# Closes of quads put off to the end of the ranges, and two PSUM banks for the last sums

## The reference

```python
x = x + _L0_gnn_ref(_layernorm(x, axis=-1), src, dst, eps, W1, b1, W2, b2, gamma, beta)
x = x + _L0_ffn_ref(_layernorm(x, axis=-1)[None], gate_w, gate_b, w1, b1, w2, b2)[0]
# gnn: N=12500 nodes, E=200000 edges sorted by dst, D=256
neigh = jax.ops.segment_sum(node_feats[src], dst, num_segments=n)
h = (1.0 + eps) * node_feats + neigh
h = jax.nn.relu(h @ W1 + b1) @ W2 + b2          # 256 -> 512 -> 256
h = (h - mean) * rsqrt(var + BN_EPS) * gamma + beta   # over all nodes
# ffn: 8 experts, top-1 routing with a capacity, 256 -> 1024 -> 256
```

## Time and profile before

| | us |
|---|---|
| three executions | 2734.87, 2713.54, 2704.42 |
| median | 2713.54 |
| the profiled execution | 2722.03, its span 2720.3 |
| mean granted clock of TensorE | 0.858 |
| busy share | TensorE 68%, VectorE 51%, ScalarE 34%, GpSimd 57% |

### The profile page before, as it was taken

How to read it: one execution, slowest core, us unless ns; L and a number is a source line. 1 busy time by engine, 2 the same in 40 slices (tenths; PEclk the granted TensorE clock), 3 DMA queues, 4 the chain that set the end, 5 groups by cost and what they waited for, 6 DMA issues and landing times. The chain is left out here.

```text
span 2720.3 us, 35963 instructions
## 1 busy us (share of the span) xinstructions
PE 1843.1 (68%) x9315; PEld 1055.5 (39%) x9316; DVE 1386.2 (51%) x4375; ACT 911.7 (34%) x1518; POOL 1553.5 (57%) x1530
## 2 busy tenths in 40 slices
PE   0035456767858878676787765557764888979996
PEld 0012223333424444333343433334332555646664
DVE  8834544545544443334342322223664676858886
ACT  6811012323323333223221110102553555545553
POOL 1266665665565666556565654650445566847775
PEclk9966678888779889889898877788887999989998
DMA  7653335656658766575677422421662322140220
GB/s 228 226 186 106 108 86 178 206 187 193 222 181 264 241 201 203 189 232 192 211 250 252 137 79 69 128 82 58 212 196 87 101 81 79 34 144 22 92 89 21
DMA packets 228639, 411.91 MB, mean 151 GB/s; under 512 B 46469, under 2 KB 110299, under 8 KB 228406
## 3 DMA queue, kind: packets, MB, share of 16 engines
q1 hardware_dynamic: 164742, 243.58, 27.4%
q0 software_dynamic: 61520, 164.41, 19.8%
q10 hardware_dynamic: 2144, 1.05, 0.1%
HBM read 338.06 MB, written 75.06 MB: 152 GB/s over the span
## 5 line engine op out<-in xcount | busy, mean ns | idle before, releaser
L948 POOL DMA_INDIRECT space<-table,space x1083 | 1036.6, 957 | 719.4 <-issue 310.2
L1043 PE MATMUL e_sums<-space 128*128 128x256 f16 x1728 | 258.3, 314 | 175.5 <-DVE space L1327 168.9
L2007 POOL TENSOR_TENSOR space<-space 128x512 f16<-128x512 f32 x200 | 296.8, 1510 | 105.3 <-ACT space L2141 100.8
L1316 DVE SCALAR_TENSOR_TENSOR space<-e_sums,above,space 128x256 f32 x141 | 68.2, 484 | 553.4 <-remote 391.5
L1043 PEld LDWEIGHTS e_sums<-space 128*128 128x128 f16 x1728 | 194.7, 113 | 239.4 <-issue 189.4
L1117 PE MATMUL e_up<-e_hT,edge_weights 128*128 128x512 f32 x384 | 211.9, 688 | 88.4 <-ACT e_hT L1218 57.3
L2097 PE MATMUL x_down<-space 128*128 128x256 f16 x2208 | 250.7, 276 | 15.9 <-DVE space L2234 15.6
L2073 PE MATMUL x_up<-space 128*128 128x512 f16 (+1 forms) x1200 | 253.1, 371 | 2.9 <-ACT space L2141 2.9
L1212 ACT ACTIVATE space<-e_tally 128x392 f32 (+1 forms) x193 | 104.9, 543 | 447.7 <-PE e_tally L1082 144.4
L2141 ACT ACTIVATE space<-x_up,b_two 128x512 f32<-128x512 f32 (+1 forms) x400 | 248.6, 691 | 17.3 <-PE x_up L2073 11.8
L1082 PE MATMUL e_tally<-w2f 128*128 128x490 f16 x343 | 136.3, 472 | 161.7 <-DVE w2f L1371 121.7
(11 more groups left out here) (230 smaller groups left out, 2522.3 us busy)
## 6 DMA issues: line engine op xcount, KB each, us to landing
w1f<-table SPq DMA_DIRECT2D x490, 256.0 KB
counts<-in_x SPq DMA_DIRECT2D x48, 512.0 KB, 4.6
space<-table,space POOLq DMA_INDIRECT x1083
slot_rows<-space SPq DMA_DIRECT2D x64, 268.0 KB
space<-slot_rows SPq DMA_DIRECT2D x32, 536.0 KB, 7.3
table<-space SPq DMA_DIRECT2D x25, 512.0 KB, 3.0
out<-space SPq DMA_DIRECT2D x24, 512.0 KB
w1f<-in_w SPq DMA_DIRECT2D x8, 1024.0 KB, 5.2
```

What stands on the lines that cost most here:

```text
L948: pool.indirect_dma_start(got[:, r, t, :], None, table.rearrange("p h d -> (p h) d"), bass.IndirectOffsetOnAxis(ap=idx[:, h, first + t:fir ...
L1043: ins = nc.tensor.matmul(sums[:, 0, 0:D], hot[:, place, t, :], got[:, r, t, half * D:(half + 1) * D], start=(t == 0 and half == 0), stop=( ...
L2007: nc.gpsimd.tensor_tensor(midl[:, j % 2, c, :], midf[:, c % MB, :], midh[:, j % 2, c, :], ALU.subtract).then_inc(s_mlo, 1)
```

## The change

`SINGLE` goes from 108 to 120, so groups 108 to 119 leave the loop. The rule for the number of quarters in a slot changes: one in most slots until the last unit is spread, two if more than three quads wait, and after the last spread four while quads wait, three otherwise. `TENSOR_ROOM`, which limits tiles and pieces beside them, goes from 1120 to 1000. `sums` gets two banks; the second is at the same time the bank of `product`, whose last use is in slot 106. In the loop TensorE waits only for the add before the last one, and VectorE reads the other bank. In `stage_norm` the block words lie in two places instead of one.

```diff
@@ -57,7 +57,7 @@
 HG = _group
 WIDE_GROUP = GROUP_OF[WIDE]
 
-SINGLE = 36 * RG
+SINGLE = 40 * RG
 NG = -(-(ET - HT) // GT)
 NIT = -(-NG // RG)
 EP = HT + NG * GT
@@ -94,7 +94,7 @@
 OWN_CLOSE = {0: 4, 1: 8, 2: NU - 1}
 CLOSE = {3: 20, 4: 29, 5: 38, 6: 45, 7: 53, 8: 59, 9: 66, 10: 72, 11: 78, 12: 83, 13: 89, 14: 94, 15: 99, 16: 104,
          17: 108, 18: 113, 19: 117, 20: 122, 21: 126, 22: 130, 23: 134}
-TENSOR_ROOM, VECTOR_ROOM, BEHIND = 1120, 960, 300
+TENSOR_ROOM, VECTOR_ROOM, BEHIND = 1000, 960, 300
 BACK, LENT_FROM, LENT = 105, 18, QT * D * 13 // 2
 LENDS = 4
 FILLED = 3 * (1 - NU % 2)
@@ -118,7 +118,7 @@
                 waiting += [q for q, u in OWN_CLOSE.items() if u == spread]
                 spread += 1
             due = min([at_slot for at_slot in CLOSE.values() if at_slot > slot] + [slot + H1C])
-            n = H1C if slot >= NG - 1 else 3 if waiting or spread == NU or len(quarters) > 2 * (due - slot) else 2
+            n = H1C if slot >= NG - 1 or spread == NU and len(waiting) > 0 else 3 if spread == NU else 2 if len(waiting) > 3 else 1
             self.quarters[slot], quarters = quarters[:n], quarters[n:]
             if self.quarters[slot] and not quarters:
                 self.weigh[slot + 2] = self.quarters[slot][-1][0]
@@ -127,7 +127,8 @@
                 self.turn[slot] = q
                 quarters = [(q, i) for i in range(2 * H1C)]
                 if slot < NG - 1:
-                    self.quarters[slot], quarters = [None, *quarters[:2]], quarters[2:]
+                    n = n if spread == NU and len(waiting) > 0 else min(n, 2)
+                    self.quarters[slot], quarters = [None, *quarters[:n]], quarters[n:]
             vector = 350 + 220 * (slot in self.spread) + 60 * (slot in self.fold) + 140 * (slot in self.weigh)
             tensor = 240 + 120 * (slot in self.turn) + 185 * sum(part is not None for part in self.quarters[slot])
             n = 0
@@ -156,7 +157,7 @@
 ORDER = [q for _, q in sorted(SLOTS_OF.turn.items())] + [NQ - 1]
 LATE = range(NG, SLOTS_OF.end)
 BORROWER = NU - 2
-assert sorted(ORDER) == list(range(NQ)) and max(SLOTS_OF.spread) < NG - 2 and max(SLOTS_OF.turn) == NG - 2
+assert sorted(ORDER) == list(range(NQ)) and max(SLOTS_OF.spread) < SINGLE and max(SLOTS_OF.turn) == NG - 2
 assert max(s for s, u in SLOTS_OF.spread.items() if u == BORROWER) < BACK and CW * HI // 2 <= LENT
 
 
@@ -438,7 +439,7 @@
         gmini = halves.lend(I32, HG)
         spans = sb("n_spans", [P, NG], F32)[:, :]
         spani = sb("n_spani", [P, NG], I32)[:, :]
-        blocki = weights[:, WORDS:WORDS + 2 * NG].bitcast(I32).rearrange("p (a g) -> p a g", a=2)
+        blocki = [weights[:, WORDS:WORDS + NG].bitcast(I32), rest[:, HT + 2 * NP:HT + 2 * NP + NG].bitcast(I32)]
         high = rest[:, HT:2 * HT].bitcast(I32)
         WRONGS = (HT - 1, HG, HT - 16, NG, NU, 1, SINGLE, 2, 1)
         wrong = [ends[:, sum(WRONGS[:i]):sum(WRONGS[:i + 1])] for i in range(len(WRONGS))]
@@ -681,30 +682,30 @@
...
-                also(nc.vector.tensor_copy(least[:, :], blocki[:, 0, :]))
+                also(nc.vector.tensor_copy(least[:, :], blocki[0]))
...
@@ -789,9 +790,9 @@
         rel = sb("e_rel", [P, 2, GT], F32)
         some = sb("e_some", [P, 2, PT], I32)
         somef = sb("e_somef", [P, PT], F32)
-        sums = psum("e_sums", [P, 1, 2 * D], F32)
+        sums = psum("e_sums", [P, 2, 2 * D], F32)
         tally = psum("e_tally", [P, BANKS, 2 * D], F32)
-        product = psum("e_product", [P, 2 * D], F32)[:, :]
+        product = sums[:, 1, :]
         up = psum("e_up", [P, 2, QN], F32)
 
         def up_of(q):
@@ -1054,11 +1055,11 @@
                     with pe.Fori(0, left):
                         place = pe.snap(turn) % 2
                         pe.wait_ge(s_hot, turn)
-                        pe.wait_ge(s_add, turn)
+                        pe.wait_ge(s_add, pe.snap(pe.snap(turn) - 1))
                         pe.reg_add(turn, turn, 1)
                         for t in range(tiles):
                             for half in range(2):
-                                ins = nc.tensor.matmul(sums[:, 0, 0:D], hot[:, place, t, :],
+                                ins = nc.tensor.matmul(sums[:, place, 0:D], hot[:, place, t, :],
                                                        got[:, r, t, half * D:(half + 1) * D],
                                                        start=(t == 0 and half == 0), stop=(t == tiles - 1 and half == 1))
                         ins.then_inc(s_sum, 1)
@@ -1309,12 +1310,12 @@
                 last_group = counter(dve, "last_group", SINGLE - 1)
                 flushed = [0]
 
-                def add_window(group):
+                def add_window(group, place=0):
 
                     for b, mask in ((0, plan.above), (1, plan.below)):
                         row = blocks_of[:, block_no(dve.snap(dve.snap(last) + b)), :].rearrange("p a d -> p (a d)")
                         ins = nc.vector.scalar_tensor_tensor(
-                            out=row, in0=sums[:, 0, 0:D], scalar=mask[:, group], in1=row,
+                            out=row, in0=sums[:, place, 0:D], scalar=mask[:, group], in1=row,
                             op0=ALU.mult, op1=ALU.add)
                     return ins
 
@@ -1353,7 +1354,7 @@
                         ins.then_inc(s_hot, 1)
                         dve.wait_ge(s_sum, turn)
                         dve.wait_ge(s_add, dve.snap(dve.snap(turn) - 1))
-                        add_window(group_no(dve.snap(last_group))).then_inc(s_add, 1)
+                        add_window(group_no(dve.snap(last_group)), dve.snap(1 - place)).then_inc(s_add, 1)
                         dve.reg_mov(last, dve.snap(block + window))
                         dve.reg_mov(last_group, group)
                         dve.reg_add(turn, turn, 1)
@@ -1441,7 +1442,7 @@
                         measure(SLOTS_OF.weigh[slot])
                 dve.wait_ge(s_sum, turn)
                 dve.wait_ge(s_add, dve.snap(dve.snap(turn) - 1))
-                then(add_window(group_no(dve.snap(last_group))))
+                then(add_window(group_no(dve.snap(last_group)), dve.snap(dve.snap(dve.snap(turn) + 1) % 2)))
                 for slot in LATE:
                     if slot in SLOTS_OF.weigh:
                         measure(SLOTS_OF.weigh[slot])
```

18 lines of the change are left out of this document (9 added, 9 removed).

## The result

The changed kernel took 2813.76 us (median of 4 runs, 2810.52 to 2831.61), the kernel before in the same set 2721.82: ratio **1.0355**, 95% interval 1.0301 to 1.0408. Slower, by 92 us, and beyond the upper end of my range (2755). Three later runs of it, on two chips, gave 1.0312 (1.0277 to 1.0347), 1.0302 (1.0258 to 1.0346) and 1.0343 (1.0287 to 1.0400).

What follows compares the result with a forecast made beforehand. The prediction took TensorE, with what it waits for, to set the pace above GpSimd's floor of 10.0 us a slot. Terms of -3, 0, -18, +8 and -4 made -17: 2696 us against the median, range 2650 to 2755.

Steps and rivals of the forecast that it cites:

- Slots 0 to 19: The first stretch, whose table stays the same: within 3 us of 242.2.
- Slots 20 to 98: The middle stretch, with fewer closes and quarters but pieces in a row: -3 us, bounds -44 and +58.
- pieces in a row: In 45 slots of the middle with one part, nothing hides the pieces' landing: +16.5 us.
- The relief in the same term: In the middle, three fewer closes give -9.5 us; 25 fewer quarters up to 35 us, only where TensorE ends the slot.
- Rival B: In the middle TensorE's work ends the slots, so the 35 us pass too: 2655 us, chance 0.22.
- Rival C: Pieces in a row starve TensorE in slots 24 to 98: +58 us there, 2757 us in all, chance 0.17.
- Rival D: Thinner work brings the middle's clock from 0.86 to 0.82: +36 us there, 2733 us in all, chance 0.16.
- Slots 99 to 105: Five more pieces, three fewer quarters and the last unit's fold as before: 0 us.
- Slots 106 to 119: Two slots hold a quad in 20.5 us, plus stalls: 166 us against 183.7, so -18, bounds -40 and 0.
- I carry two, 23 us: In slots 106 to 119, two long stalls between transposes and e_hT were counted, 23 us on top of 143.
- Slots 120 to 129: Nine quarters and a close more: +8 us, between 0 if hidden in TensorE's idle time and 17.5.
- Two banks: From slot 120 on, TensorE's wait for VectorE's add goes: -4 us, bounds -18 and 0.

Runs made afterwards that it cites:

- split3: The changed kernel with its table, but a slot's pieces and counts always split over three parts: ratio 1.0090, slots 20 to 98 in 1020.7 us.
- old_table: The kernel before with its rule of quarters and TensorE's room, plus 120 single groups and two banks for the last sums: ratio 0.9861, in a repeat 0.9908.
- hold: The changed kernel, but GpSimd issues the group two further than a transposing slot, from 109 to 119, only once the transposes are done: ratio 1.0256.
- set 2: Four edited kernels run on a chip of another kind, with prompt signals, where the kernel before took 2304.1 us.
- single_only: The kernel before with 120 single groups and one bank for the last sums: ratio 1.0010.
- old_fine: The kernel before with 120 single groups, two banks and each part split once more: ratio 0.9980, in a repeat on another chip 0.9893.
- set 1: The first four edited kernels, run on a chip with late signals, where the kernel before took 2726.3 us.
- bunched: The kernel before with its own table, but in each slot all quarters, then all pieces, then all counts: ratio 1.0523, slots 20 to 98 in 1130.9 us.

## Why the prediction was wrong

- **Slots 0 to 19**, forecast 0: 241.4 for 242.2 us. Right.
- **Slots 20 to 98**, forecast -3, measured +84.1. This step failed, in its term for the pieces in a row: +16.5 us, "+0.8 for about 15 of the first kind, +0.15 for 30 of the second". The rows cost 77.8 us here (changed against split3; 64 to 67 by the other three traces of the changed kernel) and 116.5 with the old number of quarters. I worked the row out from one slot at a clock of 1.00, in a stretch of 259 GB/s, where counts and a quarter did hide in the transfers' time, and I let the counts follow at 0.3 us each. Slot 68 shows what that left out: counts in a row become a chain over TensorE, ScalarE and VectorE at 1 to 1.6 us each, both helpers idle before it while the pieces trickle in. The clock of the stretch was 0.81 beside it. The row of counts, whose chain I hadn't priced at all, costs 51.2 us alone, the row of pieces 69.3.
- **The relief in the same term** (25 quarters fewer, up to 35 us, of which the -3 holds nothing, and three closes fewer, 9.5 us, which it holds): nothing of it shows. split3, with the thinned load and broken rows, took 1020.7 us, old_table with all of the quarters 1010.0. If the quarters that went had ended slots, split3 would be the shorter one. Rival B is out.
- **Rival C** named the mechanism, the place and the point: the wait for pieces passed 150 (163.8). Its price of +58 is near the 69.3 of the row of pieces alone; as the counts were not in it, it was too low for the whole. **Rival D**'s sign was there (0.81), but the clock followed the rows: split3 ran the same load at 0.85.
- **Slots 99 to 105**, forecast 0: +1.7. Right.
- **Slots 106 to 119**, forecast 166 us, measured 210.3. The step that failed is "I carry two, 23 us", the size of the term for late signals: six lags of the transposes came to 46.4, and the late result of slot 107 put 10.5 more before its turn, 57 in all. The 20.5 us of a quad were nearly right: without their lags the quads took 21.3 to 22.5, some 10 us over seven. 143, 57 and 10 make 210, as measured. So these fourteen slots are 34 us over my sum by late signals and 10 by the quads themselves. The 25 to 26 us of a quad in hold are no measure of a quad without lags, since the downs' signals were late there. In the other three traces of the changed kernel the stretch has 195.0 to 205.1 us, with 37 to 42 us of transposes' lags in slots 109 to 119. My price was of a close at the end of the kernel, where GpSimd had nothing left to gather. That 166 is close to old_table's 165.5 is chance: it has five closes, not seven.
- **Slots 120 to 129**, forecast +8, measured -3.9, with nine more quarters: they went into TensorE's idle time, the 0 of my bounds. Part of this is luck: the trace before has a lag of 7.7 us behind the transposes of slot 122, the changed one 0.04 in all three of its turns there.
- **Two banks**, forecast -4: 130 to the last window fell by 13.2, within its bounds. The wait for VectorE's add went from 17.9 us to none, as I had said; the 3.6 us that are left are for its one-hots. Two traces of different tables don't price the banks; the traces of the old rule put them at 192.3 to 198.4 against 183.6 to 190.1 us from slot 120 on. In set 2 the stretch from 120 on is 153.0 with one bank (single_only) and 153.2 with two (old_fine): nothing. The Trainium skill ("TensorE: Matmul & The Clock Gate", "HAM oscillation") would have had it at nothing; that chip agrees, and the other chips, by these two ranges, don't.
- **"The forecast fails most easily if the stalls of ten microseconds fall in other numbers"**: they did, 57 us for the 23 that I carried, but the whole stretch is 26.6 of the 89.6 us; the order in the middle is the larger.

## What to carry to other kernels

Work that an engine does between its waits for a small ring of buffers is not load, it is cover: before you thin it or move it, look at what stands between the fourth and the fifth transfer afterwards. When a planner's table changes a slot's number of parts, look at the order that comes out of it, since all that was split by parts is bunched with it; here one padded list gave back 78 us in the middle and 62 of the whole (2813.8 to 2751.6). Price a stage by rows of the same neighbourhood: a close with no gathers beside it gave nearly the right work (20.5 for 21.3 to 22.5 us), but none of the late signals of a close among them. And when a delay goes from where you fought it, look for it behind the next signal before you read the rest as the price of the work.

## What the runs showed of the hardware

**TensorE's signals can come long after the end in the trace, on some chips.** I compared, from 140 to 1500 us, each update of the windows' semaphore in the trace with the recorded end of the window's last matmul: in the median 2.5 us late in set 1 (old_table), 0.01 us in set 2 (single_only); for the transposes 1.2 and 0.01. In set 1's trace many updates are missing (of ScalarE and VectorE up to 60% of a line's, in set 2 hardly one). Where each update that is there is set against the last recorded end before it, ScalarE's and VectorE's lines all have medians of 0.01 us on both chips, so it is TensorE's completion that is late. Not all of TensorE's is: by the same reckoning its ups and downs have a median of 0.015 us in set 1, with a quarter to a third of them over 0.1 us late. The kernel before took 2304 us on the one chip and 2705 to 2726 on the others, and slots 0 to 19, with the same instructions, 194.4 us against 243.0. The Trainium skill ("Perfetto Trace Analysis", "Tensor Engine Instruction (MATMUL, LD_WEIGHTS)") says that the end shown for TensorE is computed from the instruction's size, and that the update goes out when PSUM has acknowledged; a lag between the two is thus possible, and these runs show its size. On the chips with late signals, hold shows that the transposes' signal is prompt once GpSimd stands still, and that the downs', which then fall under its gathers, become late. Not every signal beside a gather is late: in slot 107 of the changed kernel the gathers began with the transposes, at 1598.5 us, and the copy came 0.04 us behind them. What in the gathers does it, why only on some chips, and whether it is the array, PSUM or the signal that is held up, stays open.

**Busy time grew without work.** With the same work in the middle (3115 instructions of TensorE), TensorE was busy for 733.2 us in the kernel before and for 787.2 in bunched; the clock granted was 0.86 and 0.84. The windows (177.1 to 199.4 us) and the counts (164.9 to 184.5 in three groups) grew, the quarters shrank (217.4 to 198.7). The busy time of an engine that waits often can thus depend on the order of its waits; how much of it is the clock was not separated.
